# Loading and converting the down-projection weight: from a casting DMA of GpSimd's queue to a plain DMA and a copy on ScalarE

## The reference

```python
lam = sigmoid(u @ Wl.T + bl)
Bu  = u @ Wb.T
h_t = lam_t * h_{t-1} + Bu_t            # scan over time
x   = layernorm(u + H @ Wc.T + u * Dp)
gate, up = x @ (w_gate/127).T, x @ (w_up/127).T
out = layernorm(x + (silu(gate) * up) @ (w_down/127).T)
```

## Time and profile before

| | |
|---|---|
| median of 3 runs | 1841.45 us (1840.67 to 1844.67) |
| the profiled execution | 1843.83 us |
| its span, core 0, the slowest | 1842.3 us |
| spans of the 8 cores | 1826.5 to 1842.3 us |
| second phase, core 0 | about 54 to 551 us |
| TensorE busy over the span | 78% |
| ScalarE, VectorE, GpSimd busy | 19%, 20%, 4% |

### The profile page before, as it was taken

How to read it: one execution, slowest core, us unless ns; L and a number is a source line. 1 busy time by engine, 2 the same in 40 slices (tenths; PEclk the granted TensorE clock), 3 DMA queues, 4 the chain that set the end, 5 groups by cost and what they waited for, 6 DMA issues and landing times.

```text
span 1842.3 us, 18480 instructions; the slowest of 8 cores (1826.5 to 1842.3 us)
## 1 busy us (share of the span) xinstructions
PE 1442.9 (78%) x6718; PEld 720.3 (39%) x6832; DVE 374.6 (20%) x612; ACT 357.1 (19%) x527; POOL 75.1 (4%) x141
## 2 busy tenths in 40 slices
PE   2285484662936566999996999996999996999993
PEld 1244243342422254444443444443444443444441
DVE  2212011030105564112004112004112004122003
ACT  2103213123043353111002111002111002111001
POOL 0000000000000000000110000110000110000110
PEclk9796595775959768999997999997999997999996
DMA  2703726526340001222222222222222222222121
GB/s 69 170 24 109 154 80 134 118 74 137 64 126 1 1 1 57 75 78 77 75 70 85 75 79 76 75 70 85 75 79 76 70 73 86 75 75 80 47 74 51
DMA packets 84007, 142.76 MB, mean 77 GB/s; under 512 B 32208, under 2 KB 33232, under 8 KB 83920
## 3 DMA queue, kind: packets, MB, share of 16 engines
q1 hardware_dynamic: 35152, 70.27, 13.0%
q0 software_dynamic: 17472, 52.44, 12.5%
q10 hardware_dynamic: 31296, 18.88, 3.5%
HBM read 133.17 MB, written 27.26 MB: 87 GB/s over the span
## 4 chain that ended last, share of the span: by engine, by line
PE 67%; DMA 11%; DVE 8%; ACT 7%; issue 5%; ACTq 1%; DVEq 0%; SPq 0%; POOLq 0%; POOL 0%
PE pp L637 36%; PE pp L675 15%; PE pp L441 5%; PE pp L463 4%; DMA wdT_s<-stgw 3%; DMA wbufd<-wdT_s 3%; ACT stg L282 2%; DMA utok<-u_pre 2%; DVE stat L224 2%; PE pp L277 2%; PE pp L405 2%; PE pp L219 1%; DVE res L688 1%; ACT t2b L556 1%; DVE usum L553 1%
## 5 line engine op out<-in xcount | busy, mean ns | idle before, releaser
L637 PE MATMUL pp<-x1lo,wbufg 128*128 128x512 bf16 x768 | 295.1, 384 | 7.3 <-DMA wbufu<-wuT_s 5.5
L675 PE MATMUL pp<-hh_lo,wbufd 128*128 128x512 bf16 x768 | 290.9, 379 | 2.3 <-issue 0.5
L637 PE MATMUL pp<-x1lo,wbufu 128*128 128x512 bf16 x768 | 291.1, 379 | 1.7
L675 PE MATMUL pp<-hh_hi,wbufd 128*128 128x512 bf16 x738 | 279.4, 379 | 7.7 <-DMA wbufd<-wdT_s 6.0
L637 PE MATMUL pp<-x1hi,wbufg 128*128 128x512 bf16 x736 | 282.8, 384 | 0.0
L637 PE MATMUL pp<-x1hi,wbufu 128*128 128x512 bf16 x736 | 278.9, 379 | 0.0
L647 DVE TENSOR_TENSOR hhf<-g_sb,pp 128x512 f32<-128x512 f32 x96 | 66.1, 688 | 454.7 <-PE pp L637 454.7
L277 PE MATMUL pp<-idbf,cvgu 128*128 128x128 bf16 x384 | 48.3, 307 | 102.9 <-ACT stg L282 102.9
L653 ACT ACTIVATE hh_hi<-hhf 128x512 bf16<-128x512 f32 x96 | 60.4, 630 | 345.4 <-DVE hhf L647 345.4
L675 PEld LDWEIGHTS pp<-hh_hi,wbufd 128*128 128x128 bf16 x768 | 74.8, 97 | 122.2 <-issue 41.5
L219 PE MATMUL pp<-id,res 128*128 128x128 f32 x256 | 59.1, 396 | 77.4 <-DVE res L688 34.3
(11 more groups left out here) (72 smaller groups left out, 1187.2 us busy)
## 6 DMA issues: line engine op xcount, KB each, us to landing
wbufg<-wgT_s SPq DMA_DIRECT2D x96, 256.0 KB, 2.6
wbufu<-wuT_s SPq DMA_DIRECT2D x96, 256.0 KB, 2.7
wbufd<-wdT_s POOLq DMA_DIRECT2D x96, 256.0 KB, 2.9
utok<-u_pre SPq DMA_DIRECT2D x16, 512.0 KB, 4.6
utok<-u_main SPq DMA_DIRECT2D x16, 512.0 KB, 3.6
out<-x1tok POOLq DMA_DIRECT2D x16, 512.0 KB, 2.9
cvwd<-wd POOLq DMA_DIRECT2D x8, 768.0 KB, 17.9
cvgu<-wg POOLq DMA_DIRECT2D x6, 1024.0 KB, 16.8
```

The lines of the kernel that those rows point to most:

```text
L637: lambda e: e.matmul(o, l, r, start=st_, stop=sp_)))(
L675: lambda e: e.matmul(o, l, r, start=st_, stop=sp_)))(
```

## The change

The wd item's load leaves GpSimd's queue. SyncE loads the int32 rows as they are into a new tile `natwd` (128x3072 int32, 1.5 MB, one buffer), and ScalarE copies that tile to the bf16 tile `cvwd`, converting it. The gu4 items keep their casting DMA. Nothing is changed in the order of the items, in the transposes, or in the stores.

```diff
                     sl = dc % 2
-                    sc.step("gpsimd", (lambda d, s: (lambda e: e.dma_start(out=d, in_=s)))(
-                        cv_wd[sl][:, :], wd_h[dc * P:(dc + 1) * P, :]),
-                        writes=[("cvwd", sl)], sem=f"qx{sl}", n=16)
+                    nat_wd = bufs["nat_wd"]
+                    sc.step("sync", (lambda d, s: (lambda e: e.dma_start(out=d, in_=s)))(
+                        nat_wd[:, :], wd_h[dc * P:(dc + 1) * P, :]),
+                        writes=["natwd"], sem=f"qx{dc % 2}", n=16)
+                    sc.step("scalar", (lambda d, s: (lambda e: e.copy(out=d, in_=s)))(
+                        cv_wd[sl][:, :], nat_wd[:, :]),
+                        reads=["natwd"], writes=[("cvwd", sl)]),
...
                 cv_gu=[PE2(nc.sbuf_tensor(f"cvgu{k}", [P, 4 * D], BF16)) for k in range(2)],
+                nat_wd=PE2(nc.sbuf_tensor("natwd", [P, HID], I32)),
                 cv_wd=[PE2(nc.sbuf_tensor(f"cvwd{k}", [P, HID], BF16)) for k in range(2)],
```

## The result

The change made the kernel slower: 1860.08 us (median of 8 runs, 1857.94 to 1861.48) against 1841.55 (8 runs, 1838.48 to 1844.67), a ratio of 1.0098, 95% interval 1.0087 to 1.0109. The forecast was 1835.7, with a range of 1823 to 1848. In some executions the cores of one die show a lower granted clock and take some per cent longer (1920.43 us in one of the kernel before, clock 0.838 on the one die and 0.88 on the other); medians and ratios leave these out. The rows of before are of core 0. Lines behind L294 have moved: 401 became 406, 301 became 305, 307 became 311, 310 became 314.

The account below looks back on a forecast made before the run. Most of the chain is feed-forward matmuls; the change touches store and `utok` waits, set by full DMA engines. -8 - 16.5 + 12.1 + 1.6 + 5 = -5.8 us gave 1838.0 profiled, 1835.7 as median; range 1823 to 1848.

Parts of the forecast that it names:

- Two casts leave the first `emit_A0`: First emit_A0: two wd casting loads fewer in a full DMA stretch, 8 us saved, bounds 5 and 13.
- One cast leaves slices 1 to 3: Second wd item's store wait in slices 1 to 3: 5.5 us saved in each, 16.5 us in all.
- comes a stage early: Slice 4's first plain load: no emit_A0 precedes that slice, so it is issued one stage sooner and is there in time.
- It ends before 184 us: Slice 1, second item's plain load: issued at about 171 us into a quiet stretch, 5.2 us of DMA.
- The copy: ScalarE's int32 conversion of natwd: 2.74 us, 4.0 us from its start to the first stgw copy with the transposes.
- The first items: First wd item of each slice: first stgw copy later by 1.8, 2.3, 4.0 and 4.0 us, 12.1 in all.
- the hidden and exposed copies: Second items' conversions cost nothing in slices 1 to 3, 1.6 us in slice 4; first items' conversions cost time.
- The new wait: Third stgw copy of each slice's first item waits for a store beside the second item's plain load; 5 us taken.
- the conversion was not dear: Against the rival that ScalarE's int32 copies take twice 2.74 us: five exposed copies, +8 us, 1849; chance 0.06.
- rival without relief: Second items, slices 1 to 3: the 16.5 us saving fails, costs stay, +10.7 us, 1852; chance 0.12.
- the shorter first `emit_A0`: Sign in the first stage: emit_A0 at some 38 us instead of 46.
- the second item's wait: Sign at the second wd item's third stgw copy: a wait of about 7 us.

Follow-up runs that it names:

- e8: Kernel before with its casting loads, but every casting load of a slice held until its stage's matmuls begin; 1791.78 us, ratio 0.9715.
- e5: Kernel before, but only the first two down-weight loads made, later items reusing them, nothing in the place of the omitted casts; 1828.79 us, ratio 0.9923.
- e2: Changed kernel, but the plain load for slice 4's first item waits for stage 4's matmuls; 1851.77 us, ratio 1.0067.
- e3: Changed kernel, but ScalarE converts only the first half of each natwd tile and the transposes read it twice; 1851.87 us, ratio 1.0069.
- e4: Changed kernel, but the plain loads stay on GpSimd's queue at the old place, into two natwd buffers; ScalarE's copy stays; 1852.02 us, ratio 1.0071.
- e1: Changed kernel, but each later stage's first utok load waits until the matmuls of the stage before begin; 1853.63 us, ratio 1.0077.
- e10: Kernel before with a third stgw buffer; 1832.94 us, ratio 0.9943.

## Why the prediction was wrong

**What bounds the kernel.** Right. The second phase is ruled by when the 16 DMA engines are full, and the change acts through that and through ScalarE's copy. e8 shows it from the other side: nothing but the time of the casting loads was changed, and 53 us went.

**Two casts leave the first `emit_A0`: -8 us.** -6.2 us. The mechanism was right.

**One cast leaves slices 1 to 3: -16.5 us.** Alone it is -12.2 us (e5). In the changed kernel D1 and D2 got 5.0 and 4.9 us, close to the 5.5 taken, but D3 rose by 1.2. Here a step failed. The prediction notes that the last slice's load "comes a stage early" and counts it as being there in time. It did not ask where it lands: in the full stretch of slice 3, in the very place of the cast that was taken out. e2 takes it out of there and gets 5.7 us.

**"It ends before 184 us", and the queue behind it.** True and of no use. The prediction looked whether the plain load would reach the full stretch, and whether the `utok` loads behind it would be late. Both harmed something else: the 256 KB stores of the first item.

**The copy: 2.74 us, 4.0 with the transposes.** 2.75 us. The first items rose by 11.4 us, where 12.1 was taken, and the hidden and exposed copies are those that were named (e3, e4).

**The new wait: 0 to 2.5 us in each of four slices, 5 us taken.** 18.3 us: 6.1 in each of slices 1 and 2, 2.8 and 3.3 in slices 3 and 4. This is the term that turned the sign. The place was right and the size was not, in two ways. First, the 3.4 us of the two `utok` loads behind `natwd` on SyncE's queue were left out of what goes ahead of the store. Before the change they were issued as the stage's last tiles were transposed, and had landed when the stores began; now they start when the plain load does. e1 removes them and gets 6.9 us. Second, half of the bound was taken, as if the store got its share beside the plain load. It gets next to nothing: slices 3 and 4, with no `utok` load about, show the whole bound, 2.8 and 3.3 us. With both put right the same sum gives 4 x 2.5 + 2 x 3.4 = 16.8 us.

The trace's packet records show it. A record is one row of a transfer. Number of them that begin in the microsecond, slice 1, core 2, where the first store is issued at 166.77 and the second at 169.03:

```
us   SyncE's queue, 12288 B   SyncE's queue, 4096 B   ScalarE's queue, 256 B
     (natwd)                  (utok)                  (the stores)
167            13                       0                        0
168            22                       0                        0
169            19                       0                        0
170            23                       0                        0
171            32                       0                        2
172            14                      35                       68
173             0                      59                       56
174             0                      55                       69
175             0                      93                      101
176             0                      14                      917
177             0                       0                      832
```

Until nearly all of `natwd` is through, no row of the store moves: the first one begins 4.94 us behind the issue, where it is 0.9 us in a quiet time. The same holds on all eight cores and in all four slices: at least 98 of the 128 rows of `natwd` begin ahead of the store's first row, and at least 121 ahead of its 33rd. Then, in slices 1 and 2, come the `utok` rows, and with these the queues take turns, about one for one, though a row of the one has 16 times the bytes of the other. The store has 1024 rows of 256 B at 18 ns each, 1.1 us of work for 16 engines (the prediction took these 1.1 us without a row for them), and most of it waits until SyncE's queue is dry.

The Trainium skill (DMA: Bandwidth & Descriptors, "Queues, rings and completion order") says that an engine goes round its queues and drains a whole packet, typically some 9 to 17 descriptors, before it switches. The counts agree that queues take turns; how many rows make a turn they are too coarse to say. In the full stretches the same shows between other queues: in slice 1, from 202 to 205 us, 196 rows of GpSimd's queue and 194 of ScalarE's 1 MB stores; in slice 3, from 448 to 450 us, 37 of GpSimd's, 35 of SyncE's (12288 B) and 36 of ScalarE's. There ScalarE's queue was already moving when `natwd` came. Why the first item's store gets no turn beside `natwd` no run here shows.

**The rivals.** Most of the wrong way came by none of them. The relief came in slices 1 and 2, and the conversion was not dear. Of the rival without relief one clause came true, in slice 3 alone: "the new load falls into the full stretch". What was missing was a rival in which the new wait is long. It stood in the text as a term, with a bound that was too low. Of the signs that were named, the shorter first `emit_A0`, the second item's wait (6.41 us for about 7) and the idle time for `natwd` came. The third copy of the first item, named with 1 to 2 us, waited 8.71.

**The sum by parts.** Forecast -8 + 12.1 + 5 - 16.5 + 1.6 = -5.8 us; found -6.2 + 11.4 + 18.3 and, for the second items, -5.0 - 4.9 + 1.2 + 1.9 = +16.7. Of the 22.5 us between them the new wait is 13.3, slice 3's second item 6.7, and the rest 2.5.

What stays open: ScalarE is held at the issue of a store (11.35 us in the kernel before, 10.81 in e10) where earlier stores of its own queue have not drained, but not always: in slice 3 of the kernel before the issue at 436.51 took 0.37 us, with two 1 MB stores and a small one still on their way. That it is a limit of what one queue can have outstanding was not tried.

## What to carry to other kernels

A transfer that is moved "into a quiet stretch" has to be held against every small transfer that lives there, and with it goes all that its queue carries behind it. Count the rows, not the bytes: a store of many short rows issued behind loads of long rows was served last here, and if a buffer is reused behind it, that is a stall. And before converting by hand what the DMA converts, try to move the DMA: the same loads, held until a stretch in which the DMA engines idle, were worth 53 us here.

## What was not expected of the hardware

- A 256 KB store in rows of 256 B took 2.3 us in a quiet time and some 10.8 us (issued at 166.77, waited for until 177.66) beside 2.6 MB of loads in rows of 12 and 4 KB.
- Beside the 12288-byte rows of a load issued 2.4 us ahead of it, this store moved no row at all for 4.9 us; beside 4096-byte rows it moved about one for one.
- An engine can be held by the mere issue of a DMA: 0.37 us as a rule, 3.50, 10.81 and 11.35 us in places where its own queue was backed up.
- Taking away the buffer that a late store blocked gave back 18 us of the changed kernel, but in the kernel before only some 10, as ScalarE is held at the issue of a store there with two buffers and with three.
